# Scores in two halves between the two groups of weight transposes, in six layers of local attention

## What is computed

```python
for i in range(DEPTH):                     # DEPTH = 6
    x = attn_layer(shift_tokens(x), Wqkv[i], q_scale[i], k_scale[i], Wo[i]) + x
    x = ffn_layer(shift_tokens(x), ln_g[i], ln_b[i], W1[i], b1[i], W2[i], b2[i]) + x
...
sim = jnp.einsum('bhwie,bhwje->bhwij', bq, bk2) * QK_SCALE   # 16 heads of 64, windows of 32 rows, 64 keys each
sim = jnp.where(mask, -jnp.finfo(sim.dtype).max, sim)
attn = jax.nn.softmax(sim, -1)
out = jnp.einsum('bhwij,bhwje->bhwie', attn, bv2)
```

## Time and profile before

| | |
|---|---|
| median of 3 runs | 2795.24 us (2786.54 to 2795.59) |
| the profiled execution, its own time | 2796.39 us |
| its span, first to last instruction | 2794.6 us |
| PE busy | 2536.1 us, 91% |
| POOL busy | 1823.6 us, 65% |
| DVE busy | 1735.9 us, 62% |
| ACT busy | 1456.7 us, 52% |

### The profile page before, as it was taken

The page is one execution under the profiler, slowest core; times in us unless marked ns, Lnnn a source line. Parts: engine busy times, 40 slices in busy tenths (PEclk is TensorE's granted clock), DMA queues, the critical chain, the costliest instruction groups (busy, mean ns, idle before and its releaser), DMA issues. The chain is left out here.

```text
span 2794.6 us, 97330 instructions
## 1 busy us (share of the span) xinstructions
PE 2536.1 (91%) x40447; PEld 1723.9 (62%) x40447; DVE 1735.9 (62%) x3455; ACT 1456.7 (52%) x2654; POOL 1823.6 (65%) x3086
## 2 busy tenths in 40 slices
PE   6858999997799999999999999999999998699976
PEld 1226888895466666666666666666666666245544
DVE  6831232212677777777777777777777775476714
ACT  4722232211456666666666666666666665235532
POOL 0035666611998889888988898889888885113321
PEclk9977898955899999999999999999999999889977
DMA  1001111102121122212221222122211111000000
GB/s 34 0 23 39 38 40 28 43 16 107 56 58 46 48 63 67 65 48 63 67 65 48 63 67 65 49 66 69 68 48 48 46 48 36 26 3 4 4 2 16
DMA packets 113247, 124.87 MB, mean 45 GB/s; under 512 B 40990, under 2 KB 71342, under 8 KB 112046
## 3 DMA queue, kind: packets, MB, share of 16 engines
q1 hardware_dynamic: 112814, 118.69, 15.4%
HBM read 35.80 MB, written 8.91 MB: 16 GB/s over the span
## 5 line engine op out<-in xcount | busy, mean ns | idle before, releaser
L1727 POOL TENSOR_TENSOR l_rot_a<-l_rot_a,l_rot_b 128x512 f32<-128x512 f32 x384 | 482.8, 1277 | 32.9 <-DVE l_rot_b L1587 32.5
L1581 DVE TENSOR_TENSOR l_rot_a<-l_A,l_tab 128x512 f32<-128x512 f32 x384 | 264.3, 688 | 293.1 <-ACT l_sq L1449 270.4
L1220 PE MATMUL l_A<-l_wts,l_H 128*128 128x512 f32 x768 | 400.9, 605 | 14.9 <-DMA l_maskb<-in_l_mask 10.1
L1736 POOL TENSOR_TENSOR l_qk<-l_rot_a,l_rn 128x512 f32<-128x512 f32 x384 | 388.5, 1044 | 21.8 <-POOLq L1774 21.5
L1455 ACT ACTIVATE l_pT<-l_T 128x512 f32<-128x512 f32 x192 | 106.6, 595 | 427.0 <-PE l_T L1266 427.0
L1449 ACT ACTIVATE l_sq<-l_A 128x512 f32<-128x512 f32 x384 | 232.1, 604 | 112.4 <-PE l_A L1220 107.3
L1587 DVE TENSOR_TENSOR l_rot_b<-l_A,l_tab 128x512 f32<-128x512 f32 x384 | 260.9, 679 | 0.0
L1591 DVE TENSOR_REDUCE l_ss<-l_sq 128x8 f32<-128x512 f32 x384 | 259.1, 675 | 0.0
L1319 PE MATMUL l_T<-ident,l_qk 128*128 128x128 f32 x1536 | 209.5, 278 | 25.2 <-POOL l_qk L1736 18.6
L1319 PEld LDWEIGHTS l_T<-ident,l_qk 128*128 128x128 f32 x1536 | 172.7, 141 | 89.3 <-issue 57.1
L1799 POOL TENSOR_TENSOR l_pn<-l_sd,l_rs 128x1024 f32<-128x1024 f32 x96 | 183.1, 1907 | 38.9 <-DVE l_rs L1609 38.8
(11 more groups left out here) (340 smaller groups left out, 5630.9 us busy)
## 6 DMA issues: line engine op xcount, KB each, us to landing
l_vw<-l_vn SPq DMA_DIRECT2D x384, 128.0 KB
l_vw<-l_vn SPq DMA_DIRECT2D x360, 64.0 KB
l_wts<-in_l_wts SPq DMA_DIRECT2D x18, 650.0 KB, 4.9
c_lower_out<-c_amt SPq DMA_DIRECT2D x16, 384.0 KB, 2.5
c_inv<-c_first_in SPq DMA_DIRECT2D x16, 384.0 KB, 3.4
l_tab<-in_l_tables SPq DMA_DIRECT2D x6, 1024.0 KB, 5.1
l_wts<-in_l_wts SPq DMA_DIRECT2D x6, 635.5 KB, 4.9
result<-x SPq DMA_DIRECT2D x4, 256.0 KB, 2.3
```

The costliest lines, as they stand in the source:

```text
L1220: pe.matmul(A[j % 2][:], cols(m), w_of(m)[:, C_QKV + 512 * j:C_QKV + 512 * j + 512], start=True, stop=True).then_inc(pq_done, 1)
L1581: dve.tensor_tensor(rot_a[p][:, j, :].rearrange("p (a d) -> p a d", d=DH), src.rearrange("p (a d) -> p a d", d=DH), table[:, a, t:t + 1, : ...
L1727: pool.tensor_tensor(rot_a[m % 2][:, j, :], rot_a[m % 2][:, j, :], rot_b[:, j, :], ALU.add).then_inc(rot_rdy, 1)
L1736: pool.tensor_tensor(qk[:, j, :].rearrange("p (a d) -> p a d", d=DH), rot_a[p][:, j, :].rearrange("p (a d) -> p a d", d=DH), rn[p][:, 8 * ...
```

## The change

In each slot, `turn_probs` half 1 of tile n-1 now comes first, then the first 4 of the 8 pairs of heads of `scores` for tile n, then `turn_probs` half 0, then the other 4 pairs. No instruction is added or taken away, and no wait is changed; the waits stand with their pieces. `scores` raises `s_done` after its last pair, as before. The other engines' lists are untouched.

```diff
--- before.py
+++ after.py
@@ -1402,11 +1402,14 @@
                     narrow(group_at(n, 4))
                 if has(n - 2):
                     output(n - 2)
-                if has(n):
-                    scores(n, range(HP))
                 if has(n - 1):
                     turn_probs(n - 1, 1)
+                if has(n):
+                    scores(n, range(HP // 2))
+                if has(n - 1):
                     turn_probs(n - 1, 0)
+                if has(n):
+                    scores(n, range(HP // 2, HP))
                 if has(n + 2):
                     project(n + 2, 2)
                 if has(n - 1):
```

## The result

| | before | after |
|---|---|---|
| median, 4 runs each | 2792.01 us (2786.54 to 2795.59) | 2858.12 us (2832.2 to 2863.38) |
| ratio, 95% interval | 1 | 1.0233 [1.0197, 1.0269] |
| span of the profiled execution | 2794.6 us | 2853.3 us |

The kernel is slower by 2.3%, 66 us. The forecast was 2864 us in 2824 to 2890, slower with a chance of 0.90: right, and close. Part of the closeness is luck: of the parts that make up the sum, some were too large, some too small, and one was missing.

A forecast was written before the change was run, and what follows sets the result against it. PE, busy 96.6%, was taken as the bound. Losses of 3.7 us per four-slot cycle less 0.6 cover gave 67 us over 21.5 cycles, plus 2 for other slots: 2864 us as median, range 2824 to 2890.

The forecast's parts named there:

- The bound and the prize: PE's list sets the pace; before `values` at most 0.09 us is held, read as switch price, so almost nothing to gain.
- Rival 3: Faster: the weight loads' 73.4 us wait before `values` is real for PE and goes, giving 2756 us; chance 0.05.
- PE's own cost: On PE, splitting the scores into two blocks of 64 adds switches costing 0.19 us in each slot with no wait.
- Rival 2: Dear switches: each added edge shows a whole small matmul of 0.22, 0.25 us more per slot, 2885 us; chance 0.07.
- The late end of the scores: `s_done` comes 1.12 us later, delaying DVE, ACT and POOL behind it, and PE by an amount depending on the slot.
- The gather slot: ACT's copy of the turned outputs ends late for the next `output`; PE loses 0.28 us in this slot.
- The norm slot: ACT runs almost without gap from `exps` to `keep_v`, for which `turn_norm` waits; PE moves by 1.08 us.
- The gates slot: ACT loads a table before `exps`, then runs without gap to `keep_v`, ahead of PE's `linears`; PE moves by 1.1 us.
- The moments slot: Second half of scores stands behind half 0's wait for `add_back`, 0.85 us; with 0.39 from ACT's late `square` 0, 1.24.
- Cover by stalls: Existing stalls in `values`, 0.29 us per slot, hide as much delay in gather and norm slots: -0.6 us per cycle.
- Rival 4: About the same: ACT's delay absorbed, and issue stalls in `values` gone as two shorter blocks feed easier, 2802 us; chance 0.05.

The follow-up runs named there:

- e3: Kernel before, PE's list unchanged, with DVE's row maxima held until both groups of transposes are done: 2806.87 us, ratio 1.0066.
- e4: Changed kernel with DVE's `moments` moved behind `soft_shift`: 2835.71 us, ratio 1.0137 to the kernel before.
- e2: Changed kernel reordered so each half of scores stands ahead of its group of transposes: 2815.73 us, ratio 1.0075 to the kernel before.
- e1: Changed kernel with scores whole again, between the two groups of transposes: 2802.89 us, ratio 1.0055 to the kernel before.
- e5: Changed kernel with project part 2 moved between half 0 of the transposes and the second half of scores: 2921.81 us, ratio 1.0471 to the kernel before.
- e6: Kernel before with DVE's `moments` moved behind `soft_shift`: 2786.84 us, ratio 0.9987.
- e12: New PE order: scores, `output`, half 1, project 2, half 0, project 3, `values`; ACT's `square` 2 between its copies: 2826.53 us, ratio 1.0111 to the kernel before.
- e8: Kernel before with the first group of `turn_qk` moved ahead of `values`: 2825.89 us, ratio 1.0126.

## Why the prediction was right, and where it was not

**The bound and the prize.** Right. The way from the last project product to `values` is 0.52 before and after (2235.05 + 0.53 to 2236.10). ACT's 73.4 us were no wait of PE: they went, and nothing was gained. Rival 3, faster, fell at the point the prediction gave for it.

**PE's own cost, 0.19 per slot.** Sign and place right, size wrong: 0.36, or 31 us instead of 16. The term that was mis-sized is the way out of a small block. I had taken the project pair behind it at its usual 0.43 per product; its first now takes 0.53 (2235.05 to the second product; the pair's 1.13 against 1.02). The transposes behind a small block lose 0.05 as counted, and each block of 64 takes 0.64 to its last start where I had 0.61. The estimate made from the Trainium skill, TensorE: Matmul & The Clock Gate, Part 2, 0.33 for an added pair of switches, is nearer to this number. In the traces the 0.36 is made of three parts: 0.09 for one more way in, 0.16 for one more way out, and 0.10 in the project pair. Rival 2 named the direction of the error in PE's term, but with 0.25 more where 0.17 came.

**The late end of the scores.** The delay of `s_done` came as computed, and DVE's maxima now wait 2.00 in the gather slot and 1.76 in the norm slot; `exps` is idle 0.86 behind DVE in both. But what it cost PE was over-sized. The gather slot has 0.04 beside edges and stalls, where 0.09 was said. The norm slot was to move by 1.08 and moved by 0.90. The mechanism holds there: `keep_v`, for which `turn_norm` waits, also ends 0.90 later after `output` (11.78 against 10.88). Less of the delay reaches it, since `keep_outputs` already stood 0.30 behind `exps` before, waiting for `values`: `exps` starts 1.02 later, `keep_outputs` 0.89. The delay alone costs 0.58 in this slot (e3), so edges and stalls have a part in the 0.90. The gates slot was to move by 1.1 and moved by 0.49, with -0.14 beside edges and stalls. The failing step there is "ACT loads a table after the subtraction and before `exps`": it stands behind it in time in the earlier trace rows, but it does not wait for it. In the changed kernel it starts ahead of the subtraction's end, and `exps` moves by 0.31 instead of 1.14. e3 delays DVE and ACT while PE's list stays, and this slot grows by 0.03, or by 0.17 beside the stalls that it lost.

**The moments slot, 1.24.** The mechanism is right and shown by e4. From `output` to the project part 0.88 was added where 0.85 was said, and another 0.10 in the project pair; the printed wait is 28.3 / 23 = 1.23 on average, not 1.6. The 0.39 that I added for ACT's `square` 0 did not show: `add_back` ends as long after `output` as before. The slot grew by 1.06.

**Cover by stalls, -0.6 per cycle.** Wrong in sign. I took the stalls in `values` as a fixed thing behind which delay can hide. They grew by 0.89 per cycle. Where they stay about as they are the hiding is real: in e3's norm slot `exps` starts 1.06 later and `keep_v` ends 0.59 later. The size also came from a row that holds 9216 of the 12288 products of `values`; by the start times the stalls are 0.40 per slot, not 0.29. Rival 4 was wrong in the same way: "two shorter blocks are easier to feed" has little for it: e2, with two shorter blocks, has nearly the stalls of before (0.34 against 0.40 per slot).

**The sum.** 67 us were predicted for slots 8 to 93, 64.2 came. By slot of the cycle, what was said and what came: gather 0.28 and 0.56, moments 1.24 and 1.06, norm 1.08 and 0.90, gates 1.1 and 0.49, and -0.6 for a cover that did not come. So the gates slot was 0.6 too long, the moments and norm slots 0.2 each, the gather slot 0.3 too short, and the cover took off 0.6 too much. The errors cancel, and that the total came within 3 us is luck.

**What stays open.** Shown: the stalls stand at the borders of packets, they grow when PE gets from one border to the next in less time (after, e1, e4, e5), and part of a removed wait comes back at them (e4, e6). Not shown is what makes PE stall at a border that it reaches late, as at 22 borders of e12 and at 5 of the 44 that e8 reaches in 3.6 to 3.8 us, and why a packet starts when it does. So the table orders the kernels in the main, but the number of stalls in a new order can't be worked out from it.

## What to carry over

Before you move an engine's work forward to fill a wait, see by the start times of its matmuls, not by the idle time of its weight loads, whether there was a wait. Many small matmuls have a second limit beside their data, the arrival of their own instructions; two blocks of them set closer together can stall more, although no work was added. A block placed behind a group that sometimes waits inherits that wait and passes it on to all who need the block, so look at what each cut piece now stands behind, in every kind of slot. And a part of a forecast that calls an idle time "cover" needs a reason why it would stay the same.

## What the runs showed of the hardware

- A switch from small 64x32 products to full-array ones goes on to cost behind the edge: the first 512-column product takes 0.53 instead of 0.43, four transposes 0.05 to 0.06 more. One more pair of switches cost 0.36 in all. The Trainium skill, TensorEngine Tiling (Array Packing), section Key Properties, says that a change of mode drains TensorE; the 0.15 of the edge itself agrees, and the time lost behind it comes on top.
- PE stands idle with no wait in dense stretches of small products: 21.5 us before and 45.0 after at a granted clock of 1.00, 84.5 in e5 at 0.99. All 504 such stalls in thirteen traces stand at one place in every 256 of its instructions. Those in `values` end 2.1 to 3.3 us after the start of a packet of 16 KB that carries 256 instructions.
- A wait taken away from PE came back in part as such stalls: of 0.675 us in e6, 0.25.
- The load of ACT's table (1.28 us) starts 0.01 after the end of the instruction before it, while the activation that needs it still waits for DVE (0.81 more in the lines shown).
